# First eight rows of the next batch's first head moved into the turn's end, second additive unit in turns with head rows

## The reference, cut to what matters

```python
x = _layernorm(x + _L0_gnn_ref(x, L0_gnn_W, L0_gnn_a, adj))
x = _layernorm(x + _L1_gnn_ref(x, adj, L1_gnn_Wh, ..., L1_gnn_beta))   # 4 heads, then one more attention
x = _layernorm(x + _L2_gnn_ref(x, adj, L2_gnn_weight, L2_gnn_a))       # additive attention
x = _layernorm(x + _L3_gnn_ref(x, adj, L3_gnn_W, L3_gnn_a))            # additive attention

# L1: scores h @ h.T of a head's projection h, masked, softmax, times h
# L2, L3: scores leaky(left[i] + right[j]), masked, softmax, times Xw
```

## Time and profile before

| | us |
|---|---|
| median of 3 runs | 5713.18 (5706.15 to 5714.59) |
| profiled execution, its own time | 5713.95 |
| its span from first to last instruction | 5712.2 |
| PE busy | 5265.8 (92%) |
| DVE, ACT, POOL busy | 4372.0, 3731.8, 1942.3 |

### The profile page before, as it was taken

The page is one execution under the profiler, slowest core; times in us unless marked ns, Lnnn a source line. Parts: engine busy times, 40 slices in busy tenths (PEclk is TensorE's granted clock), DMA queues, the critical chain, the costliest instruction groups (busy, mean ns, idle before and its releaser), DMA issues.

```text
span 5712.2 us, 132229 instructions
## 1 busy us (share of the span) xinstructions
PE 5265.8 (92%) x52922; PEld 4508.6 (79%) x52922; DVE 4372.0 (77%) x7325; ACT 3731.8 (65%) x5501; POOL 1942.3 (34%) x1724
## 2 busy tenths in 40 slices
PE   8499999999999899999999999999999999999966
PEld 6388787888878788887878878787888878788755
DVE  5677678778787877778787787878788787877866
ACT  3266557676676757667576666767576675767665
POOL 3400025133341523325241343415233252413466
PEclk9799999999999999999999999999999999999988
DMA  5200000000000000000000000000000000000000
GB/s 177 61 16 11 18 9 9 9 14 14 9 9 11 17 12 7 9 18 12 15 5 10 17 14 9 9 11 16 11 9 9 18 12 15 5 9 18 13 1 5
DMA packets 138241, 95.95 MB, mean 17 GB/s; under 512 B 96032, under 2 KB 115104, under 8 KB 137632
## 3 DMA queue, kind: packets, MB, share of 16 engines
q1 hardware_dynamic: 137632, 87.49, 6.1%
HBM read 35.55 MB, written 8.91 MB: 8 GB/s over the span
## 4 chain that ended last, share of the span: by engine, by line
PE 67%; issue 12%; DVE 6%; POOLq 6%; DVEq 2%; ACT 2%; POOL 1%; DMA 0%; SPq 0%; ACTq 0%
PE po L1067 22%; PE tp L1042 22%; PE pss L1030 9%; PE pss L1031 9%; POOLq L257 6%; DVE pt L1333 3%; DVE rows L1321 2%; PE px L988 2%; DVEq L257 1%; PE px L1055 1%; PE px L1005 1%; ACT rows L1234 1%; PE px L969 1%; PE px L1015 0%; POOL shut L866 0%
## 5 line engine op out<-in xcount | busy, mean ns | idle before, releaser
L1042 PE MATMUL tp<-ident,rows 128*128 128x128 f32 x14336 | 1948.1, 278 | 234.5 <-DVE pt L1333 193.3
L1333 DVE COPY pt<-tp 128x512 f32<-128x512 f32 x2048 | 1332.8, 686 | 921.1 <-PE tp L1042 912.1
L1234 ACT ACTIVATE rows<-rows,nm 128x2048 f32<-128x2048 f32 x896 | 1795.0, 2003 | 323.3 <-DVE nm L1321 321.2
L1042 PEld LDWEIGHTS tp<-ident,rows 128*128 128x128 f32 x14336 | 1600.9, 141 | 476.8 <-issue 308.2
L1067 PE MATMUL po<-pt,hn 128*64 128x128 f32 x28672 | 1782.8, 278 | 37.5 <-ACT ot L1195 36.3
L1067 PEld LDWEIGHTS po<-pt,hn 128*64 128x64 f32 x28672 | 1568.5, 138 | 192.4 <-issue 191.7
L1186 ACT COPY pt<-tp 128x512 f32<-128x512 f32 x1536 | 837.9, 589 | 769.7 <-PE tp L1042 760.9
L869 POOL TENSOR_TENSOR rows<-sr,mask 128x2048 f32<-128x2048 f32 x256 | 1048.7, 4098 | 514.7 <-PE tp L1042 508.4
L1030 PE MATMUL pss<-ha 128*128 128x512 f32 x2560 | 1062.9, 415 | 13.1 <-DMA ha<-hb 12.0
L1031 PE MATMUL pss<-ha,hb 128*128 128x512 f32 x2560 | 1009.5, 394 | 0.0
L1321 DVE CUSTOM_DVE_ANT_0 rows<-pss,mask,nm 128x1024 f32<-128x1024 f32 x640 | 821.7, 1284 | 88.2 <-issue 3.5
(11 more groups left out here) (108 smaller groups left out, 3220.6 us busy)
## 6 DMA issues: line engine op xcount, KB each, us to landing
hb<-ha SPq DMA_DIRECT2D x164, 128.0 KB, 2.3
ha<-hb SPq DMA_DIRECT2D x164, 128.0 KB, 2.3
adjb<-in_adj SPq DMA_DIRECT2D x32, 512.0 KB, 5.6
xin<-x SPq DMA_DIRECT2D x36, 128.0 KB, 2.5
xb<-in_x SPq DMA_DIRECT2D x16, 256.0 KB, 3.0
x<-t SPq DMA_DIRECT2D x16, 256.0 KB, 2.4
xb<-x SPq DMA_DIRECT2D x8, 512.0 KB, 4.0
out<-xb SPq DMA_DIRECT2D x32, 128.0 KB, 1.9
```

What stands on the lines that cost most here:

```text
L1042: last = nc.tensor.transpose(tp[q % 2][:, r * P:(r + 1) * P], rows[:, row.slot, jb * P:(jb + 1) * P], ident[:])
L1234: nc.scalar.activation(rows[:, row.slot, :], rows[:, row.slot, :], ACT.Exp, scale=-1.0, bias=nm[:, row.place, 1:2], accum_out=rs[:, row.pl ...
L1333: nc.vector.tensor_copy(pt[:, CH * q:CH * (q + 1), row.k % SLOTS, :], tp[q % 2][:].rearrange("p (j n) -> p j n", n=P)).then_inc(pt_dve, 1)
```

## The change

Every turn but the last takes the first eight rows of the following batch's u0 (`EARLY`) into its own end; the turn then begins with u0's other eight. `ADD2` takes turns with rows of heads throughout, as `ADD1` does. The prologue takes the first eight u0 rows before its empty steps, of which three are left (`GAP`). The last turn is a segment of its own (`LAST`, 104 rows, without tasks for a following batch; before, these ran and were used by nobody). The row buffers `nm` and `rs` are now indexed modulo 8. Tasks of u1, u2 and u3 move to earlier steps, since those heads begin eight steps earlier.

```diff
-GAP = 8
+EARLY = 8
+PLACES = 8
+GAP = 3
...
-        self.odd, self.pair, self.place = k % 2 == 1, k // 2, k % NB
+        self.odd, self.pair, self.place = k % 2 == 1, k // 2, k % PLACES
...
-    order = [pair for u, hn in ((0, 1), (1, 2), (2, 1), (3, 2)) for pair in pairs_of(u, hn)] + [None] * GAP
+    order = [pair for u, hn in ((0, 1), (1, 2), (2, 1), (3, 2)) for pair in pairs_of(u, hn)]
+    order += pairs_of(0, 1)[:EARLY // 2] + [None] * GAP
...
-    tasks += [(end + GAP - 1, name, GAT2, 1) for name in ("proj", "low", "hn")]
+    tasks += [(end + EARLY, "proj", GAT2, 1), (end + EARLY + 1, "low", GAT2, 1), (end + EARLY + 1, "hn", GAT2, 1)]
...
-def loop_order():
-
-    heads = [pair for u, hn in ((0, 1), (1, 2), (2, 1), (3, 2)) for pair in pairs_of(u, hn)]
-    first, second = pairs_of(ADD1, 0), pairs_of(ADD2, 0)
-    turns_about = [pair for both in zip(first, heads[8:16]) for pair in both]
-    return pairs_of(GAT2, 2) + heads[0:8] + turns_about + heads[16:24] + second[0:1] + heads[24:28] + second[1:2] \
-        + heads[28:32] + second[2:8]
...
+def taking_turns(first, second):
+
+    return [pair for both in zip(first, second) for pair in both]
+
+
+def loop_order(last_turn):
+
+    heads = pairs_of(0, 1)[EARLY // 2:] + [pair for u, hn in ((1, 2), (2, 1), (3, 2)) for pair in pairs_of(u, hn)]
+    following = pairs_of(0, 1)[:EARLY // 2]
+    order = pairs_of(GAT2, 2) + heads[0:8] + taking_turns(pairs_of(ADD1, 0), heads[8:16]) + heads[16:22]
+    second, heads = pairs_of(ADD2, 0), heads[22:]
+    if last_turn:
+        return order + [pair for i in range(3) for pair in [second[i]] + heads[2 * i:2 * i + 2]] + second[3:]
+    return order + taking_turns(second, heads + following) + following[len(second) - len(heads):]
...
-    for unit, firsts in ((1, (21, 27)), (2, (46, 54)), (3, (74, 77))):
+    for unit, firsts in ((1, (17, 20)), (2, (34, 42)), (3, (54, 62))):
...
-    tasks += next_head(80)
+    if not last_turn:
+        tasks += next_head(80)
...
-PROLOGUE, LOOP, EPILOGUE = prologue(), main_loop(), epilogue()
+PROLOGUE, LOOP, LAST, EPILOGUE = prologue(), main_loop(False), main_loop(True), epilogue()
...
     run(PROLOGUE)
-    for _ in range(B - 1):
+    for _ in range(B - 2):
         run(LOOP)
+    run(LAST)
     run(EPILOGUE)
```

More of the change, by code:

```diff
@@ L182, in next_head, with main_loop @@
     return tasks
-def loop_order():
-    heads = [pair for u, hn in ((0, 1), (1, 2), (2, 1), (3, 2)) for pair in pairs_of(u, hn)]
-    first, second = pairs_of(ADD1, 0), pairs_of(ADD2, 0)
-    turns_about = [pair for both in zip(first, heads[8:16]) for pair in both]
-    return pairs_of(GAT2, 2) + heads[0:8] + turns_about + heads[16:24] + second[0:1] + heads[24:28] + second[1:2] \
-        + heads[28:32] + second[2:8]
-def main_loop():
-    order = loop_order()
+def taking_turns(first, second):
[8 more added lines that the diff above has]
+    return order + taking_turns(second, heads + following) + following[len(second) - len(heads):]
+def main_loop(last_turn):
+    order = loop_order(last_turn)
     tasks = []
@@ L793, in _ @@
             for b in range(B - 1):
[L794 to L797, removed]
+                if b < B - 2:
+                    src = x1[b + 2].rearrange("(k p) d -> p k d", p=P)
+                    for c in range(2):
+                        load_chunk(src, c)
+                    follow(LOOP, src)
+                else:
+                    follow(LAST, None)
                 dst = out[b].rearrange("(k p) d -> p k d", p=P)
@@ L814, in _ @@
             for c in range(2):
-                sp.wait_ge(xin_in[c], 16 * (2 * B + 2))
-            sp.wait_ge(halves_in, 128 * ((H + 1) * B + 1))
+                sp.wait_ge(xin_in[c], 16 * 2 * B)
+            sp.wait_ge(halves_in, 128 * (H + 1) * B)
         @block.gpsimd
```

## The result

The change makes the kernel slower: 5742.2 us (median of four runs, 5738.8 to 5746.5) against 5711.3 before (four runs, 5706.2 to 5714.6), a ratio of 1.0057, 95% interval 1.0044 to 1.0070. The prediction on record was 5678, with 0.08 for slower.

What follows compares the result with a forecast made beforehand. It took PE to bound the kernel, except ADD2's run, held by POOL and DVE together. Six turns give 18 us, the last turn 7, the prologue 11: 36 off 5713.95 makes 5678, range 5646 to 5706.

Steps and rivals of the forecast that it cites:

- ADD2 in turns: In six turns, ADD2's rows alternating with head rows take 190.0 us against 192.0: 2 us less a turn.
- a new wait: the two `hn` of the next u0: At steps 89 and 93 PE waits for ACT's copy `ob`: 1.1 and 2.4 us, 3.5 a turn.
- signs of being wrong: ADD2's cycle without tasks over 21.5 us, L1284 much over 0.7, or tasks at steps 17 to 22 stalling PE.
- what it wrote down to look for: Signs in windows, turn lengths (near 664.5 us), `ob` waits, POOL's masks, last turn (near 613) and prologue, with nearly full clock.
- the clock: In ADD2's run and u3's stretch, 2.6 us of work is lost at low clock; 1 us a turn comes back.
- POOL: ADD2's costlier masks, about 1.0 us more a row, are covered in the cycles: costed at nothing, at most 8 a turn.
- Rival 3: In the turns, DVE's differences collide with POOL's masks: 9.8 us lost a turn, 5737 in all; chance 0.08.
- The tasks of u1 to u3: The same work at earlier steps costs 0, with 2 us either way.
- The last turn: Tasks for a following batch go, 5.8 us, and a shorter ADD2 run gives about 1: 7 us less.
- The prologue's end: Between u0's and GAT2's rows, early u0 rows cover the first projection's path: 11 us less.
- Rival 2: The turns give nothing, only last turn and prologue gain: 5696 us, 5704 at the prologue's dear bound; chance 0.17.
- rival 1: The idle time of ADD2's run is gained whole: 8 us a turn, 5648 in all; chance 0.2.

Runs made afterwards that it cites:

- own wait: Changed kernel with TensorE's wait for the mirror count moved in front of GAT2's first projection, so u0's first early row no longer waits: 5702.1 us, ratio 0.9979.
- both: Changed kernel with the edit of own wait, and the next u0's two `hn` value transposes one step later: 5684.5 us, ratio 0.9948 to before.
- norms later: Kernel of both, with three of four layer norm quarters behind ADD1 and ADD2 two steps later: 5648.6 us, ratio 0.9883 to before.

## Why the prediction was wrong

**What failed.** In *ADD2 in turns*, the step that lists what waits in the new order: "Last a new wait: the two `hn` of the next u0". I followed the data of each task, found u0's mirrors long landed, and took that for the wait. The code says otherwise: `dot_products` waits for a count to which every projection ahead of it in TensorE's list has added, GAT2's too. With GAT2's projection at step 100 and u0's first row at 102, this was to be read in the code and in the second listing of the order. No rival had it. The prediction put this wait at nothing without a reason. Own wait gives its price: 45 us, of which 26 are the wait. None of the prediction's own signs of being wrong came up: ADD2's cycle without tasks takes 21.2 us (the sign was 21.5), and no crowd of tasks stalled PE on `px` at steps 17 to 22. Of what it wrote down to look for, only the length of a turn and the granted clock showed it.

**The sum without that wait.** The kernel that I costed is the one with own wait: forecast 5678, measured 5702, faster than before by 0.2% where 0.6% was forecast. Its turns are 668.2 us where my sum had 664.9 (667.9 - 3), 20 us over six. By stretch, with windows cut at the rows' exponentials, means of six turns in us:

| | before | changed | own wait | both | norms later |
|---|---|---|---|---|---|
| 16 rows of ADD2 and 16 of heads, with tasks | 191.1 | 195.7 | 189.8 | 187.1 | 182.7 |
| ADD1 in turns and the head rows behind it (44 rows) | 254.8 | 257.2 | 256.7 | 256.2 | 254.7 |

(In the second row, four head rows at 5.64 are taken off the value of before, which had 48.) With the false wait gone, ADD2's stretch is within 1 us of the forecast, 190.0 less 1 for the clock; but the second turn of before, from which 192.0 was read, was dearer than the mean, so this is a gain of 1.3 and not of 3. ADD1's stretch and the head rows lose 1.9, where 0 was forecast. PE's busy time says in what form: it is 636.3 a turn against 633.9 before, so where I took 1 us a turn back from *the clock*, 2.4 more are lost. That term was read from windows of the old run alone; the cycle of ADD1 that I read happened to show 1.00, though PE waits up to 1.8 us in it.

**ADD2 in turns, the waits.** The two `hn` waits were 2.0 and 0.4 us in a turn (15.9 over twelve and all turns), against 1.1 and 2.4 forecast: less in sum, and each wrong the other way. Their true price was more than their length: 3.1 us a turn by the kernel with both edits, most of it the clock. PE is idle for 17.7 us in the stretch; less 4.4 of the false wait 13.3, against 12.0 and 4.3 in the old order's two stretches: so the interleaving gains 3 us of idle time in a turn, as the direction of the forecast had it, and lost work at the low clock takes most of it away. The forecast had PE idle for about 15 of some 212 us from step 76 to the first u0 rows' end; with own wait it is 13.0 of 213.4 in the third turn, but ADD2's part of that shows a clock of 0.96, where 1.00 or nearly was forecast.

**POOL** at nothing was right: no wait of DVE for POOL's masks of note in the changed kernel (0.7 us in the whole of steps 76 to 112). **Rival 3**, slower by collisions of differences and masks, had 5737, within 5 us of the 5742 measured, and that is luck: its mechanism is refuted. The differences (L1299) have medians of 0.68 and 0.78 us in the third turn, as before (L1284) 0.68 and 0.74, and the longest took 1.10, where this rival needed about 3.

**The tasks of u1 to u3** at 0 with 2 either way: steps 16 to 31 take 107.1 us, before 106.9. ADD1's stretch and the head rows behind it take 179.6 + 78.2 = 257.8; in the third turn of before these were 174.6 + 103.6 with four rows more at 5.64, so 255.6. That is 2.2 more, just over its bound, and the clock has its part in it: PE is busy for 167.7 us in ADD1's stretch at 0.98, for 164.6 in the fifth turn, the one whose stretch shows 1.00.

**The last turn** was forecast 7 us below its rows' price. It is 2.2 above: 665.5 - 45.1 = 620.4 against 622.6. The true wait for GAT2's mirrors there, 6.3 us, has the low clock behind it. Before, three steps lay between the second projection's step 108 and row 112 in each turn; now the last turn has 102 and 104. One step sooner gave back 7.4 in that turn. The same oversight, in a plainer form: each projection must be followed to the first row that needs it.

**The prologue's end** was right: 13.6 gained where 11 were forecast. GAT2's second projection, at step 72, takes 3.7 us at full clock, and PE has work up to the dot products.

**Rival 2**, that the turns give nothing, fits own wait's turns (668.2 and 667.9) better than my forecast does. With norms later they give 9 us a turn, which is rival 1's size: much of PE's idle time was there to be had (34.0 us a turn before, 27.7 then), but by where the tasks stand and not by the interleaving alone.

## What to carry to other kernels

Where a semaphore is waited for by a running count, a wait means all that stands ahead of it in the waiting engine's list, not what its consumer needs: when rows are moved across a producer task, go through every such count and ask which additions now stand in front of it. A wait of a few microseconds on TensorE can cost more than its length, when the granted clock falls behind it: here 6.5 us a turn for 4.4 of wait. When two kinds of rows are interleaved, the small tasks between them must be placed again, off the rows where the other engines are late; here that was worth nearly as much as the false wait cost.

## What the runs showed of the hardware

The granted clock is at one of its two levels, 2.4 or 1.2 GHz, and a window's mean shows the mix. In the changed kernel it fell behind the false wait of 4.4 us, with the first dot products behind it at 0.63 us each where they take 0.40 at 2.4 GHz. It also falls behind shorter waits, but not behind each of them. In ADD1's stretch of the third turn a wait of 2.01 us is followed by slow matmuls, one of 1.79 is not (at full clock eight transposes behind such a wait take 1.16 us, and the 32 sums after them 1.97):

```profile
2315.32 1.89 PE L1057 MATMUL tp<-ident,rows 128*128 128x128 f32 x8 [2.01 <-DVE pt L1348]
2317.14 2.76 PE L1082 MATMUL po<-pt,hn 128*64 128x128 f32 x32
...
2405.79 1.16 PE L1057 MATMUL tp<-ident,rows 128*128 128x128 f32 x8 [1.79 <-DVE pt L1348]
2406.89 1.97 PE L1082 MATMUL po<-pt,hn 128*64 128x128 f32 x32
```

Length alone does not decide it: at 2359.71 a wait of 1.80 us was followed by a fall. Nor do the waits of a whole stretch. ADD2's stretch in the third and the fifth turn of the kernel with both edits, the same instructions:

```profile
2485.00:2672.80 187.80, 174.27 (x1869) 0.98 0.05 11
3815.80:4000.60 184.80, 171.39 (x1869) 1.00 0.05 12
```

PE is idle for 13.5 and 13.4 us in them, with 12 waits for copies of 10.3 and 10.1 us and two of 2.9 for `ot` in both. The first loses 2.9 us to the clock and the second nothing. With the norms moved, PE's waits for copies shrink by 22 us in all and its busy time by a further 14 over six turns, and ADD2's stretch shows 1.00 in five turns of six. What decides whether one of these waits starts a fall stays open.
